# Attention, dense FFN and mixture of experts on one core: shared-expert outputs kept on chip, elementwise work moved between engines, a shorter row-group schedule

## The reference, cut to what matters

```python
def _performer_attn(x, wq, wk, wv, wo, omega):
    q, k, v = projections of x by wq, wk, wv
    pq = _phi(q * scale, omega)
    pk = _phi(k * scale, omega)
    kv = jnp.einsum('bhsm,bhsk->bhmk', pk, v)
    z = jnp.sum(pk, axis=2)
    num = jnp.einsum('bhsm,bhmk->bhsk', pq, kv)
    den = jnp.einsum('bhsm,bhm->bhs', pq, z)
    return (num / den[..., None]) @ wo

def attn_ref(x):
    x = _layernorm(x + _performer_attn(x), ln1_g, ln1_b)              # norm 1
    h2 = gelu(x @ w1 + b1) @ w2 + b2
    return _layernorm(x + h2, ln2_g, ln2_b)                           # norm 2

def ffn_ref(x):
    shared = silu(x @ shared_w1.T) @ shared_w2.T
    gates = softmax over the two largest of x @ gate_w.T
    selected = sum over the two experts of gate * (silu(x @ w1_e.T) @ w2_e.T)
    return shared + selected

x = x + _layernorm(attn_ref(_layernorm(x)))                           # norm 0, norm 3
x = x + _layernorm(ffn_ref(_layernorm(x)))                            # norm 4, norm 5
```

## Time and profile before

| | |
|---|---|
| median of 3 runs | 606.42 us (603.66 to 609.91) |
| the profiled execution | 603.52 us, span 601.8 us |
| mean granted TensorE clock | 0.895 |
| PE, DVE, ACT, POOL busy | 465.4, 295.8, 261.4, 272.3 us |

### The profile page before, as it was taken

One profiled execution on the slowest core, in us unless ns is written; L12 is line 12 of the kernel. 1 busy time (PEld: TensorE's weight loads), 2 busy tenths in 40 slices (PEclk: granted clock), 3 DMA queues, 4 the chain that ended last, 5 costly groups with the idle time before them and its releaser, 6 DMA issues.

```text
span 601.8 us, 10616 instructions
## 1 busy us (share of the span) xinstructions
PE 465.4 (77%) x3392; PEld 360.3 (60%) x3392; DVE 295.8 (49%) x1258; ACT 261.4 (43%) x540; POOL 272.3 (45%) x408
## 2 busy tenths in 40 slices
PE   4799999999979998698625765597999899997000
PEld 3477766667655666476314544476999899887000
DVE  5887785786571477995444302300323222222273
ACT  3554544444544466554543312233444344443043
POOL 7200000110001366678878875500555655556593
PEclk9899999999999999988668877778999999999555
DMA  8920000000000000001010221345222222221621
GB/s 269 329 92 19 19 19 1 2 1 1 2 0 1 1 2 0 2 2 36 19 33 28 64 71 54 122 117 173 65 72 75 83 77 74 72 64 40 249 115 70
DMA packets 23221, 38.09 MB, mean 63 GB/s; under 512 B 4384, under 2 KB 14880, under 8 KB 22912
## 3 DMA queue, kind: packets, MB, share of 16 engines
q1 hardware_dynamic: 13248, 23.78, 12.2%
q0 software_dynamic: 4544, 9.45, 4.8%
q10 hardware_dynamic: 5376, 4.20, 2.1%
HBM read 21.74 MB, written 15.66 MB: 62 GB/s over the span
## 4 chain that ended last, share of the span: by engine, by line
PE 53%; POOL 17%; DVE 9%; another core or an unknown queue 7%; issue 6%; ACT 5%; DMA 2%; POOLq 0%; ACTq 0%; DVEq 0%; SPq 0%
POOL xs L505 5%; PE pPQ L895 4%; PE pPK L613 4%; PE pQKV L895 4%; PE pKV L688 3%; PE pPK L611 3%; PE pF L613 3%; PE pF L611 3%; PE pPK L612 3%; PE pF L612 2%; PE pQKV L811 2%; PE pPK L804 2%; POOL rs L449 2%; PE pQKV L857 2%
## 5 line engine op out<-in xcount | busy, mean ns | idle before, releaser
L578 POOL DMA_INDIRECT ys<-MID,PQT x78 | 75.7, 971 | 25.6 <-issue 25.6
L445 POOL TENSOR_TENSOR ve<-mv,eps 128x4 f32<-128x4 f32 x40 | 8.0, 201 | 164.8 <-DVE mv L1117 164.7
L505 POOL DMA_INDIRECT xs<-PL,SLOT x64 | 62.8, 981 | 19.8 <-issue 19.8
L611 PE MATMUL pPK<-XFH,E1H 128*128 128x512 f16 x32 | 15.5, 484 | 45.1 <-ACT HT L1041 25.5
L449 POOL TENSOR_TENSOR rs<-ve,halves 128x4 f32<-128x4 f32 x40 | 40.7, 1018 | 3.1
L438 POOL TENSOR_TENSOR held<-halves 128x1 f32<-128x1 f32 x47 | 9.1, 194 | 67.9 <-DVE MID L1424 58.6
L895 PE MATMUL pQKV<-E,HT 128*128 x320 | 39.1, 275 | 0.5 <-DVE MID L1424 0.5
L1424 DVE TENSOR_SCALAR MID<-pPQ,PQT 128x128 f32<-128x128 f32 x38 | 11.6, 346 | 55.7 <-remote 39.3
L895 PEld LDWEIGHTS pQKV<-E,HT 128*128 128x128 f32 x320 | 37.3, 192 | 1.0 <-issue 0.7
L895 PE MATMUL pPQ<-E,HT 128*128 x304 | 37.1, 275 | 0.4 <-DVE MID L1424 0.4
L895 PEld LDWEIGHTS pPQ<-E,HT 128*128 128x128 f32 x304 | 35.4, 192 | 0.9 <-issue 0.7
(11 more groups left out here) (258 smaller groups left out, 1309.2 us busy)
## 6 DMA issues: line engine op xcount, KB each, us to landing
PQT<-xs SPq DMA_DIRECT2D x39, 132.0 KB
PQT<-in_ew1T SPq DMA_DIRECT2D x1, 2304.0 KB, 10.7
E<-in_ew2T SPq DMA_DIRECT2D x1, 2304.0 KB, 10.6
X<-in_x SPq DMA_DIRECT2D x8, 256.0 KB, 6.0
HT<-in_ew1T SPq DMA_DIRECT2D x8, 256.0 KB, 5.9
sh<-PK ACTq DMA_DIRECT2D x8, 256.0 KB
PQT<-sh SPq DMA_DIRECT2D x8, 256.0 KB, 3.9
PQT<-ys SPq DMA_DIRECT2D x4, 512.0 KB
```

The source lines that it names most:

```text
L505: eng.indirect_dma_start(xs, bass.IndirectOffsetOnAxis(SLOT[:, g, t, a:a + 1], 0), PL[:, g, t, a, :], None).then_inc(s_scat[g], 16)
L578: eng.indirect_dma_start(ys, bass.IndirectOffsetOnAxis(XS[q][:, t, ID_AT:ID_AT + 1].bitcast(U32), 0), Y[q][:, t, :], None).then_inc(s_ysc[ ...
L611: nc.tensor.matmul(o, a[0], b_[0], start=True, stop=False)
```

## The change

Schedule: `pipeline` now takes three functions. In each of 35 steps it calls `stage` for all groups (k = step - 2n + 5), then `attend` for groups 4 to 7, then `shared` for one half of one group's shared expert.

```diff
-        STAGGER, FIRST, STAGES = 2, 5, 29
-        SHARED = 23
+        STAGGER = 2
+        FIRST, SHARED, STEPS = 5, 14, 35
+        def pipeline(attend, stage, shared):
+            for s in range(STEPS):
                 for n in range(NG):
+                    stage(n, s - STAGGER * n + FIRST)
+                for n in range(GB, NG):
+                    attend(n, s - STAGGER * (n - GB))
+                shared(*divmod(s - SHARED, 2))
```

VectorE, and POOL's order (scatters come last in a step, by `sends`):

```diff
+            def affine_stats3(n):
+                dve.wait_ge(s_no[2], n + 1)
+                y = NY[n % 2].rearrange("p (t d) -> p t d", t=T)
+                v.tensor_tensor(y, y, rows_s[:, 0, :].unsqueeze(1).to_broadcast([P, T, D]), ALU.mult).then_inc(s_n2g, 1)
+                dve.wait_ge(s_n2g, n + 1)
+                v.tensor_tensor(y, y, rows_s[:, 1, :].unsqueeze(1).to_broadcast([P, T, D]), ALU.add).then_inc(s_y2, 1)
+                hold(s_y2, n + 1, at=3)
+                stats(3, n, NY[n % 2])
+            def add_stats4(n):
+                dve.wait_ge(s_no[3], n + 1)
+                v.tensor_tensor(row(X, n), row(X, n), NY[n % 2], ALU.add).then_inc(s_x1, 1)
+                hold(s_x1, n + 1, at=4)
+                stats(4, n, row(X, n))
+            def norm4(n):
+                if n < GB:
+                    dve.wait_ge(s_free, 1)
+                else:
+                    dve.wait_ge(s_scat[n % GB], 16 * TOPK * T)
+                norm(4, n, lambda t: PL[:, n % GB, t, 0, 0:D], row(X, n))
...
+            def stage(n, k):          # POOL
                 if k == 9:
                     rstd(2, n)
                     neg_mean(2, n)
                 if k == 10:
-                    affine(n, s_no[2], NY[n % 2], NY[n % 2], rows_s[:, 3, :], rows_s[:, 4, :], s_n2g, s_y2)
-                if k == 11:
                     rstd(3, n)
                     neg_mean(3, n)
-                if k == 12:
-                    pool.wait_ge(s_no[3], n + 1)
-                    eng.tensor_tensor(row(X, n), row(X, n), NY[n % 2], ALU.add).then_inc(s_x1, 1)
+                if k == 11:
+                    rstd(4, n)
+            def sends(s):
+                for n in range(NG):
+                    if s - STAGGER * n + FIRST in (18, 19):
+                        send(n, s - STAGGER * n + FIRST - 18)
+            pipeline(attend, stage, lambda m, h: sends(2 * m + h + SHARED))
```

```diff
+                A(X2T, pT[:], ACT.Identity, scale=cols_s[:, 0:1], bias=b12[:]).then_inc(s_x1t, 1)
...
+            def down(n):
+                pe.wait_ge(s_x1t, 2 * n + 2)
+                wait(pe, s_no[2], n)
+                for t in range(T):
+                    nc.tensor.matmul(pQKV[:, t * P:(t + 1) * P], X2T[:, t * P:(t + 1) * P], ident[:],
+                                     start=(t == 0), stop=False, skip_group_check=True)
+                pe.wait_ge(s_ge, (n + 1) * FC)
...
-                    v.tensor_tensor(R2, pQKV[:], XN[:, n], ALU.add).then_inc(s_r2, 1)
```

```diff
+            def shared(m, h):
+                if 1 <= m <= NG:
+                    shared_down(m - 1, h)
+                if 0 <= m < NG:
+                    shared_up(m, h)
...
+            def shared_out(m):
+                act.wait_ge(s_sd, m + 1)
+                A(SUM[m], pPQ[:], ACT.Copy).then_inc(s_sh, 1)
...
-                    act.dma_start(sh[n].rearrange("p (c f) -> p c f", c=CH), SH[n % 2]).then_inc(s_shst[n % 2], 16)
-            for q in range(2):
-                act.wait_ge(s_shst[q], 16 * (NG // 2))
```

More of the change, by code:

```diff
@@ L148, in build @@
         MID = sb("MID", [P, 5, GW])
-        N1, R2 = (MID[:, i, :] for i in range(1, 3))
+        N1, X2T = (MID[:, i, :] for i in range(1, 3))
         NY = [MID[:, 3, :], MID[:, 4, :]]
@@ new lines, in turn_xf, with logits @@
+            def turn_xf(n):
+                pe.wait_ge(s_no[4], n + 1)
+                wait(pe, s_xfl, n)
+                turn(pKV, lambda t: PL[:, n % GB, t, 0, 0:D]).then_inc(s_fT, 1)
+            def logits(n):
+                pe.wait_ge(s_xft, n + 1)
+                pe.wait_ge(*((s_lgc, n) if n else (s_nb, 2 * NG)))
+                for t in range(T):
+                    m = nc.tensor.matmul(pF[0][:, t * E:(t + 1) * E], XFT[:, t * P:(t + 1) * P], gwT_s[:],
+                                         start=True, stop=True)
+                m.then_inc(s_lg, 1)
@@ L861, in _ @@
-            pipeline(stage)
+                    down(n)
+                if k == 12:
+                    turn_xf(n)
+                if k == 14:
+                    logits(n)
+                if k == 16:
+                    count_rows(n)
+            pipeline(attend, stage, shared)
             banks = [pF[0], pF[1], pPK[0], pPK[1]]
@@ L1055, in _, with shared @@
-            for q in range(2):
-                act.wait_ge(s_shst[q], 16 * (NG // 2))
+                    copy_row(n)
+                if k == 13:
+                    xf_turned(n)
+                if k == 15:
+                    tanh_gap(n)
+            def shared(m, h):
+                if 2 <= m <= NG + 1 and h == 0:
+                    shared_out(m - 2)
+                if 0 <= m < NG:
+                    silu(m, h)
+            pipeline(attend, stage, shared)
             banks = [pF[0], pF[1], pPK[0], pPK[1]]
@@ L1245, in _, with stats0, norm0 @@
+            def stats0(n):
+                dve.wait_ge(s_x[n % GB], 16 * (n // GB) + 16)
+                stats(0, n, row(X, n))
+            def norm0(n):
+                norm(0, n, tiles(XN[:, n]), row(X, n))
             v.memset(held[:, 0:1], 0.0).then_inc(s_batch, 1)
@@ L1367, in _, with attend @@
-            pipeline(stage)
+                    if j in (11, 13, 15):
+                        m = (j - 11) // 2
+                        dve.wait_ge(s_stage[m], 16)
+                        hold(s_stage[m], 16, at=0)
+                        split(m + 1, W1S[:, m, :])
+                if j == NT + 1:
+                    mask_kv(0)
+            copy_kv(1)
+            def attend(n, k):
+                if k == 1:
+                    recip(n)
+                if k == 3:
+                    divide(n)
+                if k == 4:
+                    res1(n, pPQ)
@@ L1368, in _ @@
+            pipeline(attend, stage, lambda m, h: None)
             dve.wait_ge(s_base, NG)
```

559 lines of the change are left out of this document (271 added, 288 removed).

## The result

The changed kernel took 646.81 us (median of 4 runs, 643.39 to 648.81), the kernel before, beside it, 606.69 (603.66 to 609.91): a ratio of 1.0655, with a 95% interval of 1.0581 to 1.0728. 617 had been predicted, with a range of 592 to 632. The direction was right, the size wrong: of the 43.9 us between the two profiled spans (645.7 and 601.8) the prediction had 13.3.

What follows compares the result with a forecast made beforehand. Bounds: PE until the first scatter, then POOL's scatters, then the shared expert. Loops to 379.2, remaining scatters 42.2, first block 5.8 later at 427.2 against 413.9: +13.3 on 603.5 gives 617 us, range 592 to 632.

Steps and rivals of the forecast that it cites:

- Loop 2: From step 15, POOL waits for its own scatters through VectorE's queue: 80.1 us for three groups, 55.6 in the old schedule.
- Loop 1: Before the scatters, hops through in-order queues make pairs of steps 17.1 us, or 18.3 to 18.8 with attention.
- D(5) to D(13): Ends of VectorE's affine and statistics in odd steps 5 to 13, before the scatters: forecast from 210.4 to 282.9 us.
- the hops in one step: Norm, affine, statistics and sum hops, formerly in separate steps, now share steps; claimed to outweigh POOL's 3.8 us relief per group.
- The shared tail ends beside this: Shared expert's last ten steps, 46 to 50 us after 379.2, end beside the scatters: priced 0, up to 3 if last.
- the 19 us that the change was to win there: Before the first expert block: the shared expert holds the blocks back by 19 us, which the change can win.
- rival C: Idle PE lowers its clock, stretching downs, halves, silus and the last shared tail, perhaps one unnamed wait: 630 us, chance 0.13.
- Outputs on chip: Beside the expert blocks, the load of the shared outputs goes: priced 0, between -3 and 0 us.
- The port that VectorE and POOL share: VectorE passes meeting POOL scatters: 24 meetings at 0.87 us could add 21 us; by queue order near 0, none added.
- Splits and turn_kv: Expert weight splits earlier in the first loop: 0 (-2 to +3); turn_kv(1) before the last features: +2, 0.5 taken.
- A: Queues overlap more than counted in both loops: end at 572 us, priced at 594, chance 0.20.
- B: PE paces the stretch before the scatters and only the later loop stands: 604 us, no change, chance 0.20.

Runs made afterwards that it cites:

- Run 1: Changed kernel with the scatters due in a step put first in POOL's program, ahead of younger groups' rstd: 618.35 us, ratio 1.0189.
- run 7: Changed kernel with scatters first, landing pauses before each four scatters (groups 4 to 7), hops spread over later steps and norm 2 one step earlier: 610.43 us, ratio 1.005.
- Run 10: Changed kernel with scatters first, landing pauses, spread hops, norm 2 early, and ACT's spread of the reciprocals one step earlier: 599.05 us, ratio 0.9851.
- Run 3: Changed kernel where POOL, for groups 4 to 7, waits before each four scatters until the four before have landed: 633.33 us, ratio 1.0451.
- runs 14: Kernel before the change with one unused 1.04 us root on POOL ahead of each four scatters of groups 4 to 7: 587.52 us, ratio 0.9691.
- 15: Changed kernel with scatters first, spread hops, norm 2 and reciprocals' spread early, one root ahead of each four scatters of all groups: 592.40 us, ratio 0.9766.
- run 5: Changed kernel with norm 2 on ACT one step earlier, ahead of the attention's copies: 646.24 us, ratio 1.066.
- run 2: Changed kernel with the hops of the second and third norm in steps of their own, routing and scatters later: 634.35 us, ratio 1.0462.

## Why the prediction was right in direction and wrong in size

**Loop 2: right.** The forecast had 29.1, 28.4 and 22.6 us from group 0 to group 3; it took 29.3, 28.0 and 21.6. POOL's gaps have VectorE's statistics as releaser, as written. Run 1 shows that POOL's order was 16 us of it.

**Loop 1: near in size, its link incomplete.** Downs 17 to 19 us apart were forecast, 16.9, 17.8, 20.5, 20.8 and 18.8 came, and the first scatter at 291.1, not 285.3. The forecast's D(5) to D(13) were 210.4, 229.2, 247.5, 265.9 and 282.9; POOL's instructions that wait for them start at 211.5, 229.2, 248.9, 269.7 and 288.5. So the start was 1 us late, the first pair gave that back, and the next three took 5.5 us too much. In these three the term that was mis-sized is PE's: the down takes 5.4 to 5.6 us where 3.8 had been put, and in two of them the residual 2.05 where 1.0 had. The granted clock was 0.72 from 227 to 233 us, 0.64 from 246 to 254 and 0.65 from 266 to 275. PE, changed kernel:

```profile
246.14 2.05 PE L777 MATMUL pQKV<-ident,MID 128*128 128x128 f32 x8 [1.49 <-ACT MID L1025]
247.98 5.56 PE L782 MATMUL pQKV<-w_s,HT 128*128 128x128 f32 x32
```

A fast down is not enough, though: run 7 has 3.74 us for it in pairs of 20.4 and 21.1 us. The forecast put this loop down to the hops in one step. Run 10 shows that the place of the spread reciprocal on ACT, which the forecast did not name, holds much of it.

**"The shared tail ends beside this ... 46 to 50 us after 379.2 ... nothing is taken for it, up to 3 if it is last": here the prediction failed.** It was last, and took 456.98 - 384.85 = 72.1 us from the end of group 3's scatters. Without its three unnamed waits, 22.7, it took 49.4, as counted. So the step that failed is the overlap: the tail was taken as hidden beside the scatters, with no held wait in it, and the 19 us that the change was to win there did not come. I had read the 30.7 us of such waits in the kernel before, and had treated them as a part of its tail that the new one would not inherit, for which only rival C kept one. They belong to a run of scatters beside PE's work, and the new schedule makes the same run: groups 3 to 5 go out without a break once VectorE no longer holds POOL. Behind ACT's held copies the slots came late as well. POOL, changed kernel:

```profile
414.89 0.19 POOL L434 TENSOR_TENSOR held<-halves 128x1 f32<-128x1 f32 x1 [9.59 <-DVE SLOT L1400]
...
428.10 0.19 POOL L434 TENSOR_TENSOR held<-halves 128x1 f32<-128x1 f32 x1 [2.70 <-DVE SLOT L1400]
```

The scatters ended at 438.6, 17.2 us later than the forecast's 421.4: these two waits are 12.3 us, 5.7 come from the later end of group 3, and the scatters themselves took 0.8 less.

The sum with what was measured: the loops end 5.7 late, the tail's own length is 49.4 where the forecast had the first block 48.0 after the loops, and 22.7 are held waits: 379.2 + 5.7 + 49.4 + 22.7 = 457.0, against the 427.2 forecast. Without the held waits it would be 434.3, 20 us later than before and still in the forecast's direction. Run 3, the test of this, has its first block at 437.97, with eight breaks in it.

**The small terms.** Blocks and tail 188.7 us: the 188 of the forecast. Outputs on chip: 2.9 us in the kernel before, nothing measurable where the scatters end last. The port that VectorE and POOL share: in 64 scatters of the changed kernel only 2 take over 1.1 us, 0.7 us too much in all. As worked out, POOL mostly waited while VectorE ran: of VectorE's 15 affine and X-sum passes after 265 us 2 meet a scatter, one without cost (295.68, scatter of 0.96) and one with 0.5 us:

```profile
375.67 0.69 DVE L1341 TENSOR_TENSOR X<-X,MID 128x512 f32<-128x512 f32 x1 [1.51 <-ACT MID L1025]
375.75 1.45 POOL L501 DMA_INDIRECT xs<-PL,SLOT  x1 [0.31 <-issue]
```

The Trainium skill's rule (SBUF — State Buffer, "SBUF: two separate sides") makes a VectorE operation with two SBUF inputs and a GpSimd operation that reads SBUF wait for each other; with the forecast's 24 meetings that gave the estimate of 21 us. The measurement decides against the count of meetings; with two of them it says little on the rule. Splits and turn_kv: the changed kernel is 1.0 us late at D(5), which bounds them together unless something else was early by as much; the filler rows stand behind the first scatter and are in the 29.3 us of the second loop, forecast at 29.1. None was tried alone.

**Rivals.** A and B needed the queues to overlap and had no share in it. C named the right ingredients (low clock, tail last, an unnamed wait) and priced them at 13 us on top of the forecast; 30 came. The right direction owes nothing to the account of the tail; it came from the two loops.

## What to carry to other kernels

A wait with no named releaser is a term, not noise: before moving work in or out of its neighbourhood, look which engine does one and the same thing without a break just until the wait ends, and break that run once as a test. Where POOL issued scatters back to back while others waited for PE, one short instruction ahead of each four was worth 3% here; the one part of the change that was tried alone was worth 0.5%. And when hops are moved between queues, list for each the instruction that it now stands behind: a wait that changes its name but not its length says that the queue, not the resource, is the bound.

## What the runs showed of the hardware

A run of scatters on POOL, one every 1.27 us, made other engines go on late with what PE had issued. With four in a row there was next to nothing (4.9 us once, with two roots; 1.2 and 1.4 us in runs 14 and 15). With eight ACT's long waits were 5.5 to 9.1 us, VectorE's up to 9.9 (run 10). With sixteen it was 13.0 (run 1) to 15.1, with twenty 13.6, 18.1 (run 5) and 20.2 (run 2); PE's own time for these products is in these figures. Most of the waits ended near the end of the run, the last of them between 1 us before and 3 us after its last scatter (361.6 and 363.4 us, 389.0 and 390.65 in the kernel before; 405.3 and 406.06, 438.6 and 440.26 in the changed one). Some ended inside it: 401.85 of 405.3 in the changed kernel, 373.92 of 377.0 in run 1.

It came after a stretch at full clock and in stretches at a lower one, with float32 and with float16 products. One 1.0 us instruction on POOL ahead of each four removed nearly all of it. Two did worse: the last scatter ended 9.1 us later (399.6 and 390.5), and 4.9 us of waits were left. What path it is that the run occupies, whether the products themselves or only their signals are late, and why two roots left a wait that one didn't, stays open: the trace records PE's products as done, and their ends are modelled. Open too are the expert blocks. There VectorE waits for the down product with no named releaser in every version, 13 times and 55.3 us together in the kernel before, at most 4.9 each, while POOL scatters the results four at a time; no run changed that.
